# Audio tower on one core: the routing mask turned by VectorE instead of TensorE, two output pairs moved, masked experts ahead of pair additions

## The chip, the cores and the metric

The kernel runs on one core of a Trainium2 chip. The metric is the time of one execution in microseconds (us), as the device counts it; of several runs the median is given. The five engines of the core are called by the names of the profile: PE is TensorE (matrix products), PEld its loading of weights, DVE is VectorE, ACT is ScalarE, POOL is GpSimd, and SP is SyncE, which here only issues DMAs.

## What is computed

There are 16 sequences (`B`) of 374 tokens with 256 channels; a 375th row of each, the readout, is used as a second input of the first projection. For every sequence:

```python
h = gelu(x_other @ W[:256] + x_readout @ W[256:] + b)          # tok
xn = layernorm(h)                                             # attention by cosine
h = h + softmax(cosine(xn, xn)) @ xn + xn
x2 = layernorm(h)                                             # routed attention
logits = normed(x2) @ normed(sim_matrix) - sigmoid(gates)     # 8 experts
mask = logits > 0, or the two largest where none is
q = sum over experts e of mask[e] * (x2 @ q_proj[e])          # k and v alike
attn = softmax(causal(q @ k.T / sqrt(128))) @ v
h = h + sum over e of mask[e] * route_w[e] * (attn @ o_proj[e])
```

The numbers are float32. The kernel makes its products from float16 halves, three products (high x high, high x low, low x high) for each.

## The kernel before

The 374 tokens of a sequence stand as 3 tiles (`NT`) of 128 partitions, the 256 channels as 2 blocks (`NC`), and there are 8 experts (`E`). All data stays on chip; the 16 sequences go through a pipeline of stages. The order on each engine is written out by hand, and engines wait for each other on semaphores. A first part takes all sequences through the tok projection. Then `pipeline` calls `step(i, g1, f, m, n)`: in one step sequence `g1` = i+1 has its first norm, `f` = i its cosine attention, second norm and routing, `m` = i-1 its q, k and v, and `n` = i-2 its causal attention and output. The steps for f = 3 to 14 are a hardware loop, the others are written out, so that 14 steps have both an `f` and an `n`; 13 of these also have a `g1`.

What matters here, in the order of a step's second half:

- **Units.** `unit(m, which, e)` on PE is the product of expert `e` for q, k or v: six matmuls of 374 columns. A step has 24, `M(0)` to `M(23)`; 16 to 23 are those of v. The unit reads `xm[:, e]`, the tokens multiplied by the expert's mask, which `mask_tokens(f, e)` writes on DVE (L1274) for the next step once the v unit of the same expert is done. In a step of both kinds, experts 0 to 4 are masked in its end and 5 to 7 in the next one's beginning.
- **Pairs.** `pair(n, p)`, p from 0 to 11, is the output product of two experts for one tile of 128 tokens: three matmuls of 512 columns into one of two banks in turn. ACT multiplies its second half by the routing weight (`scale_pairs`, L908), after which DVE adds the first half to `h` (`add_pair`, L1180). `pair(n, p)` waits on PE until the addition of pair p-2 is done (`s_pair_added`). The twelve pairs stand between units, one at a time.
- **Route.** `logits(f)` gives the logits, `route(f)` on DVE makes the mask in 16 small instructions. It writes it as float16 into `mask16`, 8 columns in each of 3 blocks of 128 (L1261).
- **Mask around.** PE turns the mask by three transposes (`turn_mask`, L1756) between unit 15 and pair 4, ACT copies the result to `maskT` (`turned_mask`, L844), SP stores it to DRAM with one DMA (L428), waits for it, and loads it back to all 128 partitions with two DMAs (L433, experts 0 to 3 and 4 to 7) into `mask_all`, which `mask_tokens` reads.
- **POOL's work beside this.** `route_weights` (L640 to L649) needs DVE's `weight_max` and `weight_sum`; then `add_tile(n, 0)` (L663, L670, L677), then `low_1(g1)` (L624, the low half of the normed tokens, 768 elements), then `add_tile(n, 1)` and `add_tile(n, 2)`. `low_1` comes after ACT's `high(0, g1)` (L787), which in turn waits for DVE's `norm_apply_tile(0, g1, 2)` (L1159). In ACT's queue `high(0, g1)` stands ahead of the scaling of pair 7.

DVE's order in the end of a step is: additions of pairs 0 and 1, `route(f)`, pairs 2 and 3, `weight_max`, low half of k, pair 4, `weight_sum`, first norm tile of `g1`, pair 5, the other two norm tiles, pairs 6 and 7, then pair 8, masked expert 0, pair 9, expert 1, pair 10, expert 2, pair 11, experts 3 and 4.

## Time and profile before

| | |
|---|---|
| median of 3 runs | 711.19 us (710.89 to 711.81) |
| profiled execution | 711.77 us, its span of instructions 710.1 us |
| PE busy | 705.5 us, 99% of the span |
| DVE busy | 579.8 us, 82% |
| ACT busy | 378.9 us, 53% |
| POOL busy | 400.5 us, 56% |
| granted TensorE clock | 1.000 of full speed |
| a step of the loop | 40.50 us |

The span is the time from the first to the last instruction. Busy shares tell only how full an engine is; what sets the time is the chain of work in which each piece waits for the one before. Times in the rows are microseconds from the start of the span. All loop steps have the same times within it, so that the rows are taken from one of them, the step that has its unit 15 at 283.68 us.

### The profile page before, as it was taken

To read this page: it belongs to the slowest core of one execution; us is meant where nothing else is said; L and a number is where in the kernel's file an instruction comes from. 1 tells how busy PE (TensorE), PEld (TensorE's weight loads), DVE (VectorE), ACT (ScalarE), POOL (GpSimd) and SP (SyncE) were. 2 spreads that over 40 slices of the span, in tenths; PEclk is the share of its full clock that TensorE was granted. 3 is DMA by queue.
4 is the path that set the end of the run, shared out by engine and by line. 5 is a ranking of instruction groups with operands and counts; after the bars stand their busy time and mean duration, and the time that the engine had idled before them with its cause. 6 is when DMAs were issued, how large, how long until landed. Compare 5 with 4: busy or idle time off the path is not lost.

```text
span 710.1 us, 18197 instructions
## 1 busy us (share of the span) xinstructions
PE 705.5 (99%) x5440; PEld 473.1 (67%) x5440; DVE 579.8 (82%) x1455; ACT 378.9 (53%) x808; POOL 400.5 (56%) x655
## 2 busy tenths in 40 slices
PE   9999999999999999999999999999999999999998
PEld 8888666675757666575756666575766657575655
DVE  5788798888879888887979888887988888886736
ACT  4977373554646364563646355464646456364443
POOL 7652325756465566746566575746566674653434
PEclk9999999999999999999999999999999999999999
DMA  9581220202020120202020020202011020201111
GB/s 246 150 188 46 74 45 8 72 3 63 14 63 14 13 65 0 71 7 63 14 55 22 9 68 0 70 8 63 14 23 55 0 71 7 63 17 46 22 68 37
DMA packets 33558, 34.35 MB, mean 48 GB/s; under 512 B 7304, under 2 KB 29304, under 8 KB 33400
## 3 DMA queue, kind: packets, MB, share of 16 engines
q1 hardware_dynamic: 33136, 33.65, 18.4%
q8 instruction: 16, 0.26, 0.2%
q10 hardware_dynamic: 392, 0.32, 0.1%
q14 instruction: 14, 0.11, 0.1%
HBM read 27.70 MB, written 6.26 MB: 48 GB/s over the span
## 4 chain that ended last, share of the span: by engine, by line
PE 98%; issue 1%; POOL 0%; POOLq 0%; DVE 0%; ACT 0%; DVEq 0%
PE bank L1671 76%; PE bank L1734 7%; PE bank L1588 5%; PE bank L1645 3%; PE bank L1577 2%; PE bank L1805 2%; PE bank L1720 1%; PE bank L1783 1%; PE bank L1593 1%; PE bank L1612 1%; PE bank L1756 0%; PE bank L1745 0%; PE bank L1748 0%; POOL region_c L670 0%; POOL region_c L663 0%
## 5 line engine op out<-in xcount | busy, mean ns | idle before, releaser
L1671 PE MATMUL bank<-xm,w_qkv 128*128 128x374 f16 x2304 | 415.7, 322 | 0.0
L1671 PEld LDWEIGHTS bank<-xm,w_qkv 128*128 128x128 f16 x2304 | 220.8, 98 | 139.2
L908 ACT ACTIVATE region_c<-bank,out_w 128x256 f32<-128x256 f32 x180 | 84.8, 471 | 163.2 <-PE bank L1671 162.2
L1274 DVE TENSOR_TENSOR xm<-xT,mask_all 128x1496 f16<-128x1496 f16 x128 | 151.9, 1209 | 0.0
L1671 PE MATMUL bank<-w_o,aoT 128*128 128x512 f16 x540 | 143.3, 379 | 0.0
L1180 DVE SCALAR_TENSOR_TENSOR h<-bank,out_w,h 128x256 f32 (+1 forms) x180 | 86.5, 481 | 48.8 <-ACT region_c L908 43.9
L663 POOL TENSOR_TENSOR region_c<-region_c 128x512 f32<-128x512 f32 x46 | 77.1, 1675 | 27.8 <-ACT region_c L908 22.8
L692 POOL TENSOR_TENSOR exp_hl<-exp,exp_hl 128x128 f16<-128x128 f32 (+2 forms) x48 | 41.9, 875 | 83.7 <-ACT exp_hl L864 83.2
L1671 PEld LDWEIGHTS bank<-w_o,aoT 128*128 128x128 f16 x540 | 50.4, 98 | 39.5
L1159 DVE TENSOR_SCALAR region_b<-h,moments,small 128x256 f32 (+1 forms) x96 | 48.8, 553 | 6.1 <-POOL small L577 6.1
L670 POOL TENSOR_TENSOR region_c<-region_c 128x256 f32<-128x256 f32 x46 | 46.9, 1019 | 8.1 <-POOL region_c L663 7.9
L1734 PE MATMUL bank<-xhl,exp_hl 128*128 128x257 f16 (+1 forms) x432 | 50.3, 272 | 0.0
L1734 PEld LDWEIGHTS bank<-xhl,exp_hl 128*128 128x128 f16 x432 | 41.6, 97 | 7.3
L677 POOL TENSOR_TENSOR h<-region_c,h 128x256 f32 (+1 forms) x45 | 37.3, 829 | 15.2 <-POOL region_c L670 10.9
L787 ACT ACTIVATE xhl<-region_b 128x768 f16<-128x768 f32 x32 | 27.0, 844 | 33.2 <-DVE region_b L1159 33.2
L817 ACT ACTIVATE region_a<-region_a,log_p,small 128x374 f32<-128x374 f32 (+2 forms) x48 | 28.2, 587 | 26.4 <-DVE region_a L1285 26.4
L573 POOL TENSOR_SCALAR small<-moments 128x3 f32<-128x3 f32 x32 | 14.4, 449 | 49.4 <-DVE moments L1151 49.4
L1671 PE MATMUL bank<-xT 128*128 128x374 f16 (+2 forms) x288 | 37.8, 268 | 0.0
L1588 PE MATMUL bank<-w_tok,xinT 128*128 128x256 f16 x288 | 37.6, 273 | 0.0
L892 ACT ACTIVATE pT<-bank 128x768 f16<-128x768 f16 x16 | 13.0, 811 | 46.0 <-PE bank L1805 46.0
L1142 DVE BATCH_NORM_STATS2 stats<-h 128x6 f32 (+1 forms) x96 | 35.7, 413 | 0.0
L587 POOL TENSOR_TENSOR small<-small,m_half 128x3 f32<-128x3 f32 x32 | 28.3, 884 | 8.1 <-POOL small L583 8.1
(200 smaller groups left out, 1067.6 us busy)
## 6 DMA issues: line engine op xcount, KB each, us to landing
mask_all<-d_mask SPq DMA_DIRECT2D x32, 384.0 KB, 3.9
h<-in_x_dram SPq DMA_DIRECT2D x16, 256.0 KB, 5.0
out_dram<-h SPq DMA_DIRECT2D x31, 128.0 KB
rnorm_row<-d_rnorm SPq DMA_DIRECT2D x16, 192.0 KB, 4.1
h<-in_x_dram SPq DMA_DIRECT2D x15, 112.0 KB, 5.4
out_dram<-h SPq DMA_DIRECT2D x15, 112.0 KB
xm<-in_L_ffn_q_proj_dram SPq DMA_DIRECT2D x2, 512.0 KB, 7.5
region_c<-in_L_ffn_k_proj_dram SPq DMA_DIRECT2D x2, 512.0 KB, 6.4
```

The lines of the kernel that those rows point to most:

```text
L663: g.tensor_tensor(prod_sum[:, 0:2, :], prod[:, buf, 0:2, :], prod[:, buf, 2:4, :], ALU.add).then_inc(s_tile_summed, 1)
L670: g.tensor_tensor(prod_sum[:, 2, :], prod_sum[:, 0, :], prod_sum[:, 1, :], ALU.add).then_inc(s_tile_summed, 1)
L677: g.tensor_tensor(h[:, n, t, :], prod_sum[:, 2, :], h[:, n, t, :], ALU.add).then_inc(s_tile_ready, 1)
L692: done = g.tensor_tensor(exp2_hl[:, 1, sl], exp2[:, sl], exp2_hl[:, 0, sl], ALU.subtract)
L908: a.activation(prod[:, prod_buf(n, t), q, :], pair_bank(n, p)[:, C:2 * C], ACT.Copy, scale=weights_out(n)[:, t, 2 * q + 1:2 * q + 2]).then ...
L1142: v.bn_stats(stats[n][:, t, :], h[:, b, t, :]).then_inc((s_stats1, s_stats2)[n], 1)
L1159: v.tensor_scalar(xs[n][:, t, :], h[:, b, t, :], moments[n][:, t, 0:1], small[n][:, 4, t:t + 1], ALU.subtract, ALU.mult).then_inc((s_xs1, ...
L1180: v.scalar_tensor_tensor(h[:, n, t, :], pair_bank(n, p)[:, 0:C], weights_out(n)[:, t, e0:e0 + 1], h[:, n, t, :], ALU.mult, ALU.add).then_i ...
L1274: v.tensor_tensor(xm[:, e, :, 0:T], xT[1][:, :, :, 0:T].rearrange("p a c t -> p (a c) t"), mask_all[:, e, 0:T].unsqueeze(1).broadcast_to([ ...
L1588: t_.matmul(projected(t), xinT[:, b % 2, xp, c, t * P:(t + 1) * P], w_tok[:, wp, c, :], start=(c == 0 and xp == 0 and wp == 0), stop=False ...
L1671: last = t_.matmul(dst, left[lp], right[rp], start=(starts and k == 0), stop=(stops and k == 2), skip_group_check=True)
L1734: last = t_.matmul(banks[t][:, 0:n], exp1_hl[:, ep, j, t * P:(t + 1) * P], xhl[0][:, xp, j, 0:n], start=(j == 0 and k == 0), stop=(j == NT ...
```

## The change

- PE no longer turns the mask, and ACT no longer copies it. `mask16` becomes a block of 128 x 32 with the 24 values (expert, tile) of a token side by side, and DVE turns it in one instruction (`turn_mask`, a transposition of blocks of 32 x 32) into `mask_turned`, after the addition of pair 2. In it the tokens of 32 partitions stand in 24 rows of a 32-partition block.
- SP stores this with four DMAs of 24 rows with 32 values each, instead of one with 8 rows of 384 values, and then loads as before, from the same layout.
- On PE, pair 4 comes after unit 16 instead of after unit 15. Each pair after it comes a unit later too, except pair 11, which stays after unit 22 and so directly follows pair 10.
- On DVE each of the masked experts 0 to 3 comes ahead of the addition of pair 8 to 11 instead of behind it.
- The zeros for PE's first matmuls, which were in `mask16`, are now in `mask_all`.

```diff
+    SQ = 32
-        mask16 = sb("mask16", [P, NT, P], F16)
-        maskT = sb("maskT", [E, TP], F16)
+        mask16 = sb("mask16", [P, SQ], F16)
+        mask_turned = sb("mask_turned", [P, SQ], F16)
...
             def mask_around(f):
                 sp.wait_ge(s_mask_row, f + 1).then_inc(s_sp_passed, 1)
-                sp.dma_start(d_mask[f, :].rearrange("(e t) -> e t", e=E), maskT[:, :]).then_inc(s_mask_stored, 16)
-                sp.wait_ge(s_mask_stored, 16 * (f + 1)).then_inc(s_sp_passed, 1)
+                rows = d_mask[f, :].rearrange("(r b j) -> b r j", r=SQ, j=SQ)
+                for q in range(P // SQ):
+                    sp.dma_start(rows[q][0:NT * E, :], mask_turned[q * SQ:q * SQ + NT * E, :]).then_inc(s_mask_stored, 16)
+                sp.wait_ge(s_mask_stored, 16 * (P // SQ) * (f + 1)).then_inc(s_sp_passed, 1)
...
-            def turned_mask(f):
-                act.wait_ge(s_mask_turned, f + 1)
-                if later(f):
-                    act.wait_ge(s_mask_stored, 16 * f)
-                a.activation(maskT[:, :], as16(turn[1] if later(f) else turn[0], TP)[0:E, :], ACT.Copy).then_inc(s_mask_row, 1)
...
+            def turn_mask(b):
+
+                dve.wait_ge(s_mask_ready, 2 * b + 1)
+                if later(b):
+                    dve.wait_ge(s_mask_stored, 16 * (P // SQ) * b)
+                v.transpose(mask_turned[:, :], mask16[:, :]).then_inc(s_mask_row, 1)
...
                     for e in range(E - 3):
+                        mask_tokens(f, e)
                         pairs(8 + e, min(9 + e, PAIRS))
-                        mask_tokens(f, e)
...
-            def turn_mask(f):
-                pe.wait_ge(s_mask_ready, 2 * (f + 1))
-                pe.wait_ge(s_T2_lo, f + 1)
-                for t in range(NT):
-                    last = t_.transpose(as16(turn[1] if later(f) else turn[0], TP)[:, t * P:(t + 1) * P], mask16[:, t, :], ident16[:, :])
-                last.then_inc(s_mask_turned, 1)
...
-                    M(15)
-                    turn_mask(f)
+                    M(15, 16)
                     pair(n, 4)
-                    for k in range(7):
-                        M(16 + k)
+                    for k in range(6):
+                        M(17 + k)
                         pair(n, 5 + k)
+                    pair(n, PAIRS - 1)
```

PE in the loop from unit 15 on, before. The units read `xm,w_qkv` (bank1 is k, bank5 is v), the pairs `w_o,aoT`:

```order
L1671 MATMUL bank1<-xm,w_qkv 128x374 x6
L1756 MATMUL bank7<-ident16,mask16 128x128 [waits T2_lo,mask_ready]
L1756 MATMUL bank7<-ident16,mask16 128x128 x2
L1835 REGISTER_ALU
L1671 MATMUL bank2<-w_o,aoT 128x512 [waits pair_added]
L1671 MATMUL bank2<-w_o,aoT 128x512 x2
L1671 MATMUL bank5<-xm,w_qkv 128x374 [waits v_lo]
```

The same place now:

```order
L1674 MATMUL bank1<-xm,w_qkv 128x374 x6
L1674 MATMUL bank5<-xm,w_qkv 128x374 [waits v_lo]
L1674 MATMUL bank5<-xm,w_qkv 128x374 x5
L1831 REGISTER_ALU
L1674 MATMUL bank2<-w_o,aoT 128x512 [waits pair_added]
L1674 MATMUL bank2<-w_o,aoT 128x512 x2
```

The three transposes are gone, and the first v unit (bank5) stands ahead of pair 4.

PE at the end of the same loop step now, from unit 22 to the turning of the next first norm:

```order
L1674 MATMUL bank5<-xm,w_qkv 128x374 x6
L1831 REGISTER_ALU
L1674 MATMUL bank2<-w_o,aoT 128x512 [waits pair_added]
L1674 MATMUL bank2<-w_o,aoT 128x512 x2
L1831 REGISTER_ALU
L1674 MATMUL bank3<-w_o,aoT 128x512 [waits pair_added]
L1674 MATMUL bank3<-w_o,aoT 128x512 x2
L1655 REGISTER_ALU
L1649 MATMUL bank6<-ident16,xhl1 128x128 [waits logits_out,hi1]
```

Pair 10 (bank2) and pair 11 (bank3) are neighbours; before, unit 22 was between them.

DVE in the loop from the addition of pair 7, before; the additions write `h`, the masked experts `xm`:

```order
L1180 SCALAR_TENSOR_TENSOR h<-bank,out_w,h 128x256 [waits pair_added,pair_scaled]
L1177 REGISTER_ALU
L1180 ISA [waits pair_scaled]
L1180 SCALAR_TENSOR_TENSOR h<-bank,out_w,h 128x256
L1273 ISA [waits T2_lo,T2_hi,mask_loaded0]
L1274 TENSOR_TENSOR xm<-xT,mask_all 128x4x374 [waits v_done]
```

and now:

```order
L1174 SCALAR_TENSOR_TENSOR h<-bank,out_w,h 128x256 [waits pair_added,pair_scaled]
L1273 ISA [waits T2_lo,T2_hi,mask_loaded0]
L1274 TENSOR_TENSOR xm<-xT,mask_all 128x4x374 [waits v_done]
L1171 REGISTER_ALU
L1174 ISA [waits pair_scaled]
L1174 SCALAR_TENSOR_TENSOR h<-bank,out_w,h 128x256
```

The wait for the loaded mask and the first masked expert moved ahead of the addition of pair 8.

## Rows read from the trace of the kernel before

**Rows 1.** The page: busy time of each engine.

```profile
PE 705.5 (99%) x5440; PEld 473.1 (67%) x5440; DVE 579.8 (82%) x1455; ACT 378.9 (53%) x808; POOL 400.5 (56%) x655
```

**Rows 2.** One loop step: its us, busy PE, PEld, DVE, ACT, POOL, PEclk.

```profile
283.68:324.18 40.50, 40.50 (x308) 26.32 (x307) 34.49 (x88) 21.23 (x46) 24.71 (x39) 1.00 0.13 34
```

**Rows 3.** Timeline of PE: start us, us, engine, line, operation.

```profile
283.68 1.11 PE L1671 MATMUL bank<-xm,w_qkv 128*128 128x374 f16 x6
284.63 0.33 PE L1756 MATMUL bank<-ident,mask 128*128 128x128 f16 x3
284.79 0.81 PE L1671 MATMUL bank<-w_o,aoT 128*128 128x512 f16 x3
...
286.39 0.81 PE L1671 MATMUL bank<-w_o,aoT 128*128 128x512 f16 x3
...
295.98 0.81 PE L1671 MATMUL bank<-w_o,aoT 128*128 128x512 f16 x3
```

**Rows 4.** Timeline of DVE in that step: pair additions, norm tiles, masked experts.

```profile
284.21 1.07 DVE L1180 SCALAR_TENSOR_TENSOR h<-bank,out_w,h 128x256 f32 x2
...
286.41 0.49 DVE L1180 SCALAR_TENSOR_TENSOR h<-bank,out_w,h 128x256 f32 x1
...
287.75 0.48 DVE L1180 SCALAR_TENSOR_TENSOR h<-bank,out_w,h 128x256 f32 x1
288.15 1.80 DVE L1159 TENSOR_SCALAR region_b<-h,moments,small 128x256 f32 x2
...
291.22 0.48 DVE L1180 SCALAR_TENSOR_TENSOR h<-bank,out_w,h 128x256 f32 x1 [0.88 <-ACT region_c L908]
...
293.13 1.02 DVE L1274 TENSOR_TENSOR xm<-xT,mask_all 128x1496 f16<-128x1496 f16 x1
...
294.54 1.53 DVE L1274 TENSOR_TENSOR xm<-xT,mask_all 128x1496 f16<-128x1496 f16 x1
296.00 0.47 DVE L1180 SCALAR_TENSOR_TENSOR h<-bank,out_w,h 128x256 f32 x1
```

**Rows 5.** Timeline of ACT in that step.

```profile
285.07 0.48 ACT L844 ACTIVATE maskT<-bank 8x384 f16<-8x384 f16 x1 [0.72 <-PE bank L1756]
...
289.98 0.84 ACT L787 ACTIVATE xhl<-region_b 128x768 f16<-128x768 f32 x1 [0.67 <-DVE region_b L1159]
290.73 0.46 ACT L908 ACTIVATE region_c<-bank,out_w 128x256 f32<-128x256 f32 x1
```

**Rows 6.** Timeline of POOL in that step.

```profile
287.37 0.31 POOL L647 TENSOR_TENSOR lg<-lg,row 128x24 f32<-128x24 f32 x1 [1.21 <-DVE row L1345]
...
288.53 1.27 POOL L663 TENSOR_TENSOR region_c<-region_c 128x512 f32<-128x512 f32 x1 [0.34 <-POOL route_w L649]
...
291.06 0.73 POOL L677 TENSOR_TENSOR h<-region_c,h 128x256 f32 x1 [0.36 <-ACT xhl L787]
291.75 1.61 POOL L624 TENSOR_TENSOR xhl<-region_b,xhl 128x768 f16<-128x768 f32 x1
293.31 1.97 POOL L663 TENSOR_TENSOR region_c<-region_c 128x512 f32<-128x512 f32 x1
```

**Rows 7.** Timeline of DVE, early in the program.

```profile
54.35 0.55 DVE L1080 SCALAR_TENSOR_TENSOR xinT<-bank,xinT 128x384 f16<-128x384 f32 x1
```

**Rows 8.** Timeline of PE at the same place.

```profile
55.04 0.92 PE L1577 MATMUL bank<-ident,h 128*128 128x128 f32 x6
```

**Rows 9.** Timeline of SP in that step: the mask's store and its two loads.

```profile
285.79 0.30 SPq L428 DMA_DIRECT2D d_mask<-maskT  x1
287.54 0.90 SPq L433 DMA_DIRECT2D mask_all<-d_mask  x2
```

**Rows 10.** SP's waits, two steps: line, source, total us, times, longest.

```profile
SPq L420 <- DMA d_rnorm<-small: 3.9, 2, 2.2
...
SPq L429 <- DMA d_mask<-maskT: 2.5, 2, 1.3
```

**Rows 11.** DMA issues from 287.00 to 287.90: KB, us to landing.

```profile
mask_all<-d_mask SPq DMA_DIRECT2D x1, 384.0 KB, 3.7
```

More of the change, by code:

```diff
@@ L101, in audio_tower_kernel @@
         row3 = sb("row3", [P, 6, NT])
-        mask16 = sb("mask16", [P, NT, P], F16)
-        maskT = sb("maskT", [E, TP], F16)
+        mask16 = sb("mask16", [P, SQ], F16)
+        mask_turned = sb("mask_turned", [P, SQ], F16)
         mask_all = sb("mask_all", [P, E, TP], F16)
+        zeros16 = mask_all[:, 0, 0:P]
         route_w = sb("route_w", [P, B, NT, E])
@@ L160, in audio_tower_kernel @@
         d_route = nc.dram_tensor("d_route", [(NT - 1) * E * P], F32, kind="Internal").ap()
-        d_mask = nc.dram_tensor("d_mask", [B, E * TP], F16, kind="Internal").ap()
+        d_mask = nc.dram_tensor("d_mask", [B, SQ * P], F16, kind="Internal").ap()
         bank = [ctx.enter_context(nc.psum_tensor(f"bank{i}", [P, 512], F32)) for i in range(8)]
@@ L259, in audio_tower_kernel @@
         s_route_exp = sem("route_exp")
-        s_mask_turned = sem("mask_turned")
         s_mask_row = sem("mask_row")
@@ L751, in _ @@
             act.wait_ge(s_pad_zeroed, 1)
-            a.activation(unused[:, :], mask16[:, 0, 0:1], ACT.Gelu)
+            a.activation(unused[:, :], zeros16[:, 0:1], ACT.Gelu)
             def split_in(b):
@@ L920, in step @@
                     head_high(qT, qkv_bank[0], s_q_done, m + 1, s_q_hi, [], qkv_out)
-                    turned_mask(f)
                     route_exp(f)
@@ L961, in step @@
                     scale_pairs(0, 4)
-                    turned_mask(f)
                     head_high(kT, qkv_bank[1], s_k_done, m + 1, s_k_hi, [(s_scores_done, NT * m)], qkv_out)
@@ L1040, in _ @@
             exp_cosines(1, (2,))
-            turned_mask(0)
             route_exp(0)
@@ L1054, in _ @@
             v = nc.vector
-            v.memset(mask16[:, 0, :], 0.0).then_inc(s_pad_zeroed, 1)
+            v.memset(zeros16, 0.0).then_inc(s_pad_zeroed, 1)
             v.memset(h[96:P, 0:1, NT - 1, :], 0.0).then_inc(s_zeroed, 1)
@@ L1064, in _ @@
             v.memset(read_hl[:, :], 0.0).then_inc(s_zeroed, 1)
-            v.memset(mask16[:, 1:NT, :], 0.0)
+            v.memset(mask16[:, :], 0.0)
             def token_weights_low():
@@ L1258, in route @@
                                              ALU.is_lt, ALU.mult))
-                if later(b):
-                    dve.wait_ge(s_mask_turned, b)
-                v.tensor_tensor(mask16[:, :, 0:E], lg[:, 0, :, :], M, ALU.add).then_inc(s_mask_ready, 1)
+                v.tensor_tensor(mask16[:, 0:NT * E].rearrange("p (e t) -> p t e", t=NT), lg[:, 0, :, :], M,
+                                ALU.add).then_inc(s_mask_ready, 1)
                 v.tensor_tensor(lg[:, 8, :, :], lg[:, 0, :, :], M, ALU.add).then_inc(s_mask_ready, 1)
                 assert at[0] == RP
+            def turn_mask(b):
[3 more added lines that the diff above has]
+                v.transpose(mask_turned[:, :], mask16[:, :]).then_inc(s_mask_row, 1)
             def mask_tokens(b, e):
@@ L1396, in step @@
                     route(f)
+                    turn_mask(f)
                     weights_low(2 * NC)
@@ L1437, in step @@
                     route(f)
-                    pairs(2, 4)
+                    pairs(2, 3)
+                    turn_mask(f)
+                    pairs(3, 4)
                     weight_max(f)
@@ L1543, in _ @@
             route(0)
+            turn_mask(0)
             weights_low(2)
@@ L1611, in _ @@
             for k in range(WARM):
-                t_.matmul(bank[6][:, 0:P], mask16[:, 0, :], mask16[:, 0, :], start=True, stop=True)
+                t_.matmul(bank[6][:, 0:P], zeros16, zeros16, start=True, stop=True)
             pe.wait_ge(s_consts, 1)
@@ L1620, in _ @@
             for k in range(FILL):
-                t_.matmul(bank[6][:, 0:P], mask16[:, 0, :], mask16[:, 0, :], start=True, stop=True)
+                t_.matmul(bank[6][:, 0:P], zeros16, zeros16, start=True, stop=True)
             pe.wait_ge(s_tok_read, 16)
@@ L1653, in turn_first_high @@
                     pe.wait_ge(s_logits_out, b)
-                    pe.wait_ge(s_mask_row, b)
                 turn_rows(0, b, 0, turn[0], s_turned1_hi)
@@ L1929, in step @@
                     pair(n, 3)
-                    M(15)
-                    turn_mask(f)
+                    M(15, 16)
                     pair(n, 4)
-                    for k in range(7):
-                        M(16 + k)
+                    for k in range(6):
+                        M(17 + k)
                         pair(n, 5 + k)
+                    pair(n, PAIRS - 1)
                     if g1 is not None:
@@ L1946, in step @@
                 pe.wait_ge(s_logits_out, B)
-                pe.wait_ge(s_mask_row, B)
                 turn_v(n)
@@ L2023, in _ @@
             turn_in(13)
-            turn_mask(0)
             dots(1, 2)
@@ L2035, in _ @@
             pe.wait_ge(s_hi2, 2)
-            pe.wait_ge(s_mask_row, 1)
             turn_rows(1, 1, 0, turn[0], s_turned2_hi)
```

## The prediction

> **What bounds the kernel now.** I read the page first. PE is busy for 705.5 us of a span of 710.1 us [rows 1]; DVE, the next, has 82%. Busy PE in the page can hide waits, because the ends of matmuls are modelled, so I went on to the view by stages and the timeline. A loop step takes 40.50 us, in which PE is busy for 40.50 us at the full granted clock of 1.00 [rows 2]. In the timeline the starts say the same: the six matmuls of 374 columns of a unit take 0.95 us from the unit's start to what follows, wherever it stands (283.68 to 284.63), and a unit and a pair take 1.60 us together (284.79 to 286.39, and seven times that to the last pair at 295.98) [rows 3]. So PE waits for nothing in the loop. Two things follow. PE work that goes away is gained in full as long as nobody else is late, and any wait of PE that is new is lost in full.
>
> **The work taken off PE.** The three transposes stand from 284.63 to 284.79, 0.16 us [rows 3]. There are 16 such groups, one for each sequence: 16 x 0.16 = 2.56 us. I take this as it stands also for the two groups ahead of the loop, which are 0.3 us of it together. ACT loses a copy, which nobody gains by, since ACT is busy for 21.23 of 40.50 us [rows 2].
>
> **DVE's transposition.** The trace shows no such operation on DVE. The nearest rows are the small operations of 24 numbers, as POOL's L647 of 0.31 us in [rows 6]; two additions of pairs 2 and 3 with nothing between take 1.07 us together, 0.10 more than twice 0.48 [rows 4], so that up to 0.1 us of it lies in a gap and the rest delays the addition of pair 3. Even at the 0.5 us of a whole addition of 256 numbers this hits nobody: pair 3 would be added by 285.8, and pair 5, the one that waits for it on PE, now starts at 287.2. Below nothing it can't be. I take 0.2 us, because 32 numbers are nearest to the small operations. It ends at 284.21 + 0.40 + 0.2 = 284.8, where 0.40 is the distance from an addition to the next independent instruction (287.75 to 288.15) [rows 4].
>
> **The new place of the pairs.** With unit 16 in front, pair 4 starts at 284.63 + 0.95 = 285.58, and pair p at 1.60 us for each later one: pair 5 at 287.18, pair 7 at 290.37, pair 8 at 291.97, pair 9 at 293.57, pair 10 at 295.17. Pair 11 follows after 0.65 us (1.60 less 0.95) at 295.81. For pair 4 this is right: the addition of pair 2 begins at 284.21 and ends about 284.7, and left where it was, pair 4 would come at 284.63 and wait. Pairs 4 to 10 are 0.79 us later than before, and with them ACT and DVE; pair 11 is 0.17 us earlier. What decides is the last: pair 11 needs the addition of pair 9, which began on PE only 2.24 us before, where it had 3.2 us. From a pair's start on PE to the start of its addition on DVE, with ACT's scaling between, are 1.36 us (286.39 to 287.75) [rows 3, 4], to its end 1.84. PE starts 0.14 us after the end of a DVE instruction that it waited for (54.90 to 55.04) [rows 7, 8]. That makes 1.98 of 2.24 us: 0.26 us to spare, if DVE is free.
>
> **Is DVE free?** Here the exchange of masked experts and additions counts. I follow the chain through the step.
>
> The additions of pairs 4 and 5 start at 286.94 and 288.54. POOL's L647 starts 0.96 us after the first (286.41 to 287.37), L663 1.16 us later [rows 4, 6], so it wants to start at 289.06. The two norm tiles on DVE start 0.40 after pair 5's addition, at 288.94. Before, L663 came 0.38 us after the first tile had started and the second tile was held up: the pair of tiles took 1.80 us and ended at 289.95, 0.15 us after L663 (289.80) [rows 4, 6]. So these instructions of DVE and POOL's additions run one at a time. Now L663 comes 0.12 us after the first tile, waits for it till about 289.2, and ends at 290.48; the second tile ends at 290.63.
>
> POOL: L677 ends 1.99 us after L663 (289.80 to 291.79), and L624 would start 0.04 before that end [rows 6]: 292.47 and 292.43.
>
> ACT: L787 starts 0.03 us after the second tile, at 290.66, the scaling of pair 7 comes 0.75 us later (289.98 to 290.73), and DVE's addition 0.49 us after that (291.22) [rows 4, 5]: 291.90. The first masked expert is then ready to start at 292.30. It finds POOL in L677 till 292.47.
>
> A masked expert that is held up ends 0.79 us after POOL's instruction: that of 294.54 ended at 296.07, L663 at 295.28. POOL, held up by DVE, gets going about 0.14 us before DVE's end: L663 ended at 295.28, its own time of 1.27 after 294.01, and the masked expert ended at 294.15 [rows 4, 6]. So masked expert 0, which has waited longer than L624, ends at 292.47 + 0.79 = 293.26. L624 then runs its 1.61 us from 293.12 to 294.73. The addition of pair 8 does not mind that: the pair additions take 0.47 to 0.49 us whatever POOL runs [rows 4]. Masked expert 1 wants to start near 293.8, waits for L624 and ends at 294.73 + 0.79 = 295.52. The addition of pair 9, now behind it, starts 0.07 us before that end (296.00 against 296.07) [rows 4] and ends at 295.92. PE starts pair 11 at 295.92 + 0.14 = 296.06 instead of 295.81: a wait of 0.25 us.
>
> This holds in the steps that have a next first norm (L624 comes from it), 13 of them: 13 x 0.25 = 3.3 us. In the last step with a route there is none. **The sum** is 711.19 - 2.56 + 3.3 = 711.9 us. I make it against the median; the profiled execution was 711.77 us with a span of 710.1, 1.7 us around it that the change leaves alone. An error of 0.1 us in the chain is 1.3 us in the time, which makes this case 710.4 to 713.8.
>
> **The mask's way over DRAM.** Masked expert 0 can start at 292.30 only if the load has landed. Before, the first store came 0.24 us after ACT's copy had ended (285.55 to 285.79) [rows 5, 9]; now it comes at 284.8 + 0.24 = 285.05. Issues of one kind are 0.5 us apart (two loads of about 0.35 took 0.90) [rows 9], so the fourth store is issued at 286.55. From a store's issue to the load's is 1.75 us (285.79 to 287.54), and the load lands 3.7 us later [rows 9, 11]: 292.0, 0.4 us before L624. The bound above is the store of the norms, 128 short rows: SP waits for it 2.2 us at the longest, for the mask's 1.3 us [rows 10]. The new stores have 24 rows of 64 bytes each, before 8 of 768. At 0.9 us more the load lands at 292.9, too late. Four small stores at once are nearer to the mask's store in rows than to that of the norms, so I take 292.0 to 292.2.
>
> The Trainium skill says in "DMA: Bandwidth & Descriptors", under Specifications, that a transfer below 512 bytes makes the DMA engine read, modify and write. That speaks against this change; by it the four stores would be slower than the row, and the case would be the second rival below. No row of before shows a store of the mask in 64-byte pieces.
>
> **First rival, PE waits for nothing.** If the masked experts 0 and 1 don't meet L624 between them, say since it keeps out of DVE's way, each takes the 0.9 to 1.0 us of an undisturbed one, the addition of pair 9 ends at 293.57 + 1.84 = 295.41, and pair 11 starts on time. Then the whole 2.56 us are gained: 708.6 us. For it: the chain has a dozen steps, and 0.26 us in it are enough. Against it: the two norm tiles and the masked expert of 294.54 were held up by POOL in just this way [rows 4], in every step of the loop.
>
> **Second rival, the load comes too late, slower.** If masked expert 0 is not ready when POOL comes to L624 at 292.43, L624 takes its turn first, till 294.04. Masked expert 0 ends at 294.83, and the addition of pair 8, which now stands behind it, at 295.23; pair 10 starts at 295.37 instead of 295.17, 0.20 late. POOL's L663 goes ahead of masked expert 1 (294.69 to 295.96), which ends at 296.75; the addition of pair 9 ends at 297.15, and pair 11 starts at 297.29 instead of 296.01, 1.28 late. Together 1.48 us in each of 13 steps, 19.2 us: 711.19 - 2.56 + 19.2 = 727.8 us. The point from which it decides is a landing about 0.4 us later than I have it. For it: the 64-byte rows and four issues where one was. Against it: the transposition and PE's and ACT's copy that no longer stand ahead give 0.7 us back.
>
> That the change does not do what it says, that is that PE's 0.16 us don't come free, has nothing for it in a PE that is full, and gets no share of its own.
>
> **How the numbers follow.** The forecast's case, 711.9 us, has 0.55; the first rival, 708.6, has 0.25; the second, 727.8, has 0.20. The range leaves out the second rival and nothing else: 708.3 to 714.5. A measurement of this kernel can tell 0.2%, 1.4 us, from no change: faster is below 709.8, slower above 712.6. Of the likeliest case 0.36 lies between, 0.17 above and 0.02 below. Of the first rival 0.23 is faster and 0.02 within. That makes 0.25 faster, 0.38 the same, 0.37 slower.
>
> **What the profile after would show.** Right: a loop step of 40.50 - 0.16 + 0.25 = 40.6 us; a gap on PE only ahead of the last pair, with DVE's addition as its releaser; the first masked expert of a step ending ahead of L624 and the second held up by it; unit 15 and unit 16 next to each other without a gap. First rival: a step of 40.34 us and no gap. Second: a step near 41.8 us, and L624 ahead of the first masked expert. The prediction is wrong if PE waits at another place, say at pair 4 or at the first units of the next step, if the order of DVE and POOL at 292.4 is another, or if PE does not give 0.16 us for each mask.

## The result: slower by 1.1%, outside the range

| | before | after |
|---|---|---|
| median of 5 runs | 711.81 us (710.89 to 712.2) | 719.94 us (718.95 to 719.99) |
| ratio | | 1.0112, 95% interval 1.01 to 1.0124 |
| profiled execution, span | 711.77, 710.1 us | 719.03, 717.3 us |
| forecast | | 711.9 us, 708.3 to 714.5 |

The change costs 8.1 us between the medians and 7.2 us between the two spans. The page of after, against [rows 1]:

```profile
PE 705.8 (98%) x5392; PEld 468.9 (65%) x5392; DVE 587.6 (82%) x1471; ACT 374.4 (52%) x792; POOL 400.6 (56%) x655
```

48 matmuls are gone, and busy PE still shows 0.3 us more. As in before, that number hides waits. Two neighbouring loop steps by stages, columns as in [rows 2]:

```profile
286.86:327.40 40.54, 40.50 (x305) 26.09 (x303) 34.32 (x89) 20.96 (x45) 24.95 (x39) 1.00 0.14 34
327.40:369.16 41.76, 40.66 (x305) 26.00 (x303) 35.82 (x89) 20.96 (x45) 24.04 (x39) 1.00 0.13 33
```

In before one step of the loop was as long as the next. Now there are two kinds, of 40.54 and of 41.76 us, at the same granted clock and with the same number of instructions. The forecast named 40.6 us for its own case and "near 41.8" for the second rival: both came true, in one execution. PE's waits by source (us in total, times, longest) point to one place:

```profile
PEld bank L1674 <- DVE h L1174: 15.4, 20, 1.6
```

L1174 is the addition of a pair. The waits of PEld overlap matmuls that still run, so I take PE's own gaps from the starts of matmuls, less the time of their columns. Below, T is the start of DVE's transposition in a step: 286.73 in the first of these two, 327.26 in the second.

**A short step.** PE from pair 9, DVE and POOL:

```profile
295.68 0.81 PE L1674 MATMUL bank<-w_o,aoT 128*128 128x512 f16 x3
296.32 1.11 PE L1674 MATMUL bank<-xm,w_qkv 128*128 128x374 f16 x6
297.27 1.67 PE L1674 MATMUL bank<-w_o,aoT 128*128 128x512 f16 x6
298.78 0.39 PE L1649 MATMUL bank<-ident,xhl 128*128 128x128 f16 x4
...
294.04 0.48 DVE L1174 SCALAR_TENSOR_TENSOR h<-bank,out_w,h 128x256 f32 x1 [0.88 <-ACT region_c L905]
294.44 0.97 DVE L1274 TENSOR_TENSOR xm<-xT,mask_all 128x1496 f16<-128x1496 f16 x1
295.63 0.48 DVE L1174 SCALAR_TENSOR_TENSOR h<-bank,out_w,h 128x256 f32 x1 [0.22 <-ACT region_c L905]
296.03 1.64 DVE L1274 TENSOR_TENSOR xm<-xT,mask_all 128x1496 f16<-128x1496 f16 x1
297.59 0.47 DVE L1174 SCALAR_TENSOR_TENSOR h<-bank,out_w,h 128x256 f32 x1
...
293.88 0.73 POOL L680 TENSOR_TENSOR h<-region_c,h 128x256 f32 x1 [0.36 <-ACT xhl L790]
294.57 2.31 POOL L627 TENSOR_TENSOR xhl<-region_b,xhl 128x768 f16<-128x768 f32 x1
```

Pairs 10 and 11 stand from 297.27 to 298.78, 1.51 us, where two pairs of 0.65 take 1.30: the gap ahead of pair 11 is 0.21. Masked expert 0 starts at 294.44, ahead of POOL's L627 (L624 in before). L627 is held up by it and takes 2.31 us instead of 1.61; masked expert 1 is held up by L627 and takes 1.64; the addition behind it ends at 298.06, and pair 11 follows.

**A long step**, the same three engines:

```profile
336.22 0.81 PE L1674 MATMUL bank<-w_o,aoT 128*128 128x512 f16 x3
336.87 1.11 PE L1674 MATMUL bank<-xm,w_qkv 128*128 128x374 f16 x6
337.96 0.82 PE L1674 MATMUL bank<-w_o,aoT 128*128 128x512 f16 x3
339.89 0.82 PE L1674 MATMUL bank<-w_o,aoT 128*128 128x512 f16 x3 [1.10 <-DVE h L1174]
...
334.58 0.48 DVE L1174 SCALAR_TENSOR_TENSOR h<-bank,out_w,h 128x256 f32 x1 [0.88 <-ACT region_c L905]
335.35 2.16 DVE L1274 TENSOR_TENSOR xm<-xT,mask_all 128x1496 f16<-128x1496 f16 x1 [0.28 <-DMA mask_all<-d_mask]
337.43 0.47 DVE L1174 SCALAR_TENSOR_TENSOR h<-bank,out_w,h 128x256 f32 x1
337.83 1.60 DVE L1274 TENSOR_TENSOR xm<-xT,mask_all 128x1496 f16<-128x1496 f16 x1
339.36 0.47 DVE L1174 SCALAR_TENSOR_TENSOR h<-bank,out_w,h 128x256 f32 x1
...
334.43 0.72 POOL L680 TENSOR_TENSOR h<-region_c,h 128x256 f32 x1 [0.36 <-ACT xhl L790]
335.11 1.61 POOL L627 TENSOR_TENSOR xhl<-region_b,xhl 128x768 f16<-128x768 f32 x1
336.68 1.97 POOL L666 TENSOR_TENSOR region_c<-region_c 128x512 f32<-128x512 f32 x1
```

Masked expert 0 now waits for the DMA that brings the mask, and POOL's L627 starts first, undisturbed (1.61). The masked expert takes 2.16 us, pair 10 starts 0.15 late (336.22 + 1.59 would be 337.81), and pair 11, 0.65 after pair 10 without a wait, comes 1.27 late.

**Which step is which kind.** By the trace the first of the two loads has landed 7.34 to 7.64 us after T in the 7 short steps and 7.74 to 7.97 in the 5 long ones of the loop. L627 comes at 7.83 to 7.86 in either; a masked expert starts about 0.1 us behind its wait. The two kinds don't overlap. The first step with both parts, ahead of the loop (T = 122.37), has the long order too, but not for the mask's sake. Its mask landed 7.01 us after T, and DVE came to the masked expert only at 7.70, when POOL had begun at 7.57:

```profile
130.07 2.27 DVE L1274 TENSOR_TENSOR xm<-xT,mask_all 128x1496 f16<-128x1496 f16 x1
...
129.94 1.61 POOL L627 TENSOR_TENSOR xhl<-region_b,xhl 128x768 f16<-128x768 f32 x1
```

Pair 11 waits 1.06 us there. Seven gaps of 0.20, five of 1.42 and this one of 1.06 make 1.4 + 7.1 + 1.1 = 9.6 us. Less the 2.56 us of the transposes, and with 0.2 us of gaps in the program's first part, this is 7.2 us, what the spans differ by. Runs of after lie at 718.95 to 719.03 and at 719.94 to 719.99; one long step in place of a short one is 1.2 us, which fits the distance of 0.96 roughly, but only one of these runs has a trace.

SP in the two steps, the short one first:

```profile
285.93 0.37 SPq L424 DMA_DIRECT2D rnorm_row<-d_rnorm  x1
287.17 1.82 SPq L431 DMA_DIRECT2D d_mask<-mask_turned  x4
290.52 0.95 SPq L436 DMA_DIRECT2D mask_all<-d_mask  x2
...
327.04 0.37 SPq L424 DMA_DIRECT2D rnorm_row<-d_rnorm  x1
327.71 1.82 SPq L431 DMA_DIRECT2D d_mask<-mask_turned  x4
331.49 0.95 SPq L436 DMA_DIRECT2D mask_all<-d_mask  x2
```

The stores start 0.44 us after T in both, as forecast (284.61 to 285.05). The loads are issued 3.79 and 4.23 us after T; over all steps it is 3.69 to 4.36, where the forecast has 3.69 for every step (288.30). L424 is the load of the norms' row, 192 KB, on the same queue just ahead of the stores. It lands 2.73 to 3.37 us after T, and in the loop steps the loads of the mask are issued 0.96 to 1.01 us behind that landing. In before the same thing varied too; the loads in two other loop steps:

```profile
247.42 0.90 SPq L433 DMA_DIRECT2D mask_all<-d_mask  x2
...
328.13 0.90 SPq L433 DMA_DIRECT2D mask_all<-d_mask  x2
```

Counted from PE's transposes (244.13, 284.63 and 325.13) these and [rows 9] are 3.29, 2.91 and 3.00 us. Over all loop steps of before it is 2.92 to 3.45, and in eleven of the twelve the loads go out 0.13 to 0.19 us behind the landing of the norms' row; in the twelfth, where that row was issued late (0.45 us behind the transposes), they go out 0.10 ahead of it. The forecast took its row from one step, and the section on the profile before said that all loop steps have the same times. That holds for the four engines that compute, not for DMAs.

### The profile page after: what moved, and what is told of

Its sections match the earlier page's. It is cut to its first block, busy times and chain, and to the rows that moved or that the text cites. A ratio compares the mean times of both kernels' runs of the same rounds, so it can differ in the third digit from the quotient of the medians.

```text
span 717.3 us, 18200 instructions
## 1 busy us (share of the span) xinstructions
PE 705.8 (98%) x5392; PEld 468.9 (65%) x5392; DVE 587.6 (82%) x1471; ACT 374.4 (52%) x792; POOL 400.6 (56%) x655
## 4 chain that ended last, share of the span: by engine, by line
PE 94%; DVE 2%; issue 2%; ACT 1%; POOL 1%; POOLq 0%; DVEq 0%; ACTq 0%
PE bank L1674 74%; PE bank L1737 7%; PE bank L1592 4%; PE bank L1649 3%; PE bank L1801 1%; PE bank L1581 1%; PE bank L1723 1%; PE bank L1779 1%; PE bank L1616 1%; PE bank L1597 1%; DVE h L1174 1%; ACT region_c L905 1%; DVE xm L1274 0%; PE bank L1751 0%; PE bank L1748 0%
## 5 line engine op out<-in xcount | busy, mean ns | idle before, releaser
L1274 DVE TENSOR_TENSOR xm<-xT,mask_all 128x1496 f16<-128x1496 f16 x128 | 158.8, 1255 | 1.0 <-DMA mask_all<-d_mask 0.8
L1174 DVE SCALAR_TENSOR_TENSOR h<-bank,out_w,h 128x256 f32 (+1 forms) x180 | 86.2, 479 | 45.5 <-ACT region_c L905 44.0
L695 POOL TENSOR_TENSOR exp_hl<-exp,exp_hl 128x128 f16<-128x128 f32 (+2 forms) x48 | 38.9, 811 | 74.1 <-ACT exp_hl L861 74.0
L627 POOL TENSOR_TENSOR xhl<-region_b,xhl 128x768 f16<-128x768 f32 x16 | 31.0, 1940 | 4.5 <-ACT xhl L790 4.5
```

What stands on the lines that cost most here:

```text
L695: done = g.tensor_tensor(exp2_hl[:, 1, sl], exp2[:, sl], exp2_hl[:, 0, sl], ALU.subtract)
L1174: v.scalar_tensor_tensor(h[:, n, t, :], pair_bank(n, p)[:, 0:C], weights_out(n)[:, t, e0:e0 + 1], h[:, n, t, :], ALU.mult, ALU.add).then_i ...
L1274: v.tensor_tensor(xm[:, e, :, 0:T], xT[1][:, :, :, 0:T].rearrange("p a c t -> p (a c) t"), mask_all[:, e, 0:T].unsqueeze(1).broadcast_to([ ...
```

## The experiments

All have the median of their batch's runs of before beside them: 711.51, 711.6, 711.52 and 711.58 us for the four batches.

### Which part of the change costs: e4, e5, e1

**e4** turns the mask on DVE and leaves the pairs and the masked experts in the order of before.

```diff
-                    M(15, 16)
+                    M(15)
                     pair(n, 4)
-                    for k in range(6):
-                        M(17 + k)
+                    for k in range(7):
+                        M(16 + k)
                         pair(n, 5 + k)
-                    pair(n, PAIRS - 1)
...
-                        mask_tokens(f, e)
                         pairs(8 + e, min(9 + e, PAIRS))
+                        mask_tokens(f, e)
```

> Only the turning of the mask is changed: on DVE instead of PE and ACT, with four stores. The pairs stand on PE as in the kernel before (pair 4 behind unit 15, unit 22 between pairs 10 and 11), and DVE's order of additions and masked experts is that of before. Theory: the only wait is that of pair 4 for the addition of pair 2, which ends 0.06 us after pair 4 could start, 0.2 us with the distance from DVE to PE, in 14 steps: 711.8 - 2.56 + 0.2 + 2.8 = 712.2 us. Rival (the four stores themselves cost the time, by coming late for the masked experts wherever the pairs stand): gaps at pairs 9 to 11 too, 716 us or more.

Measured: 710.87 us, ratio 0.9991 (0.9981 to 1.0001). PE's waits for additions:

```profile
PEld bank L1674 <- DVE h L1174: 4.7, 15, 0.3
```

Pair 4 waits 0.13 us in each loop step, as it comes 0.16 earlier and the addition of pair 2 hasn't ended; nothing else waits. 711.5 - 2.56 + 12 x 0.13 + 0.2 is 710.7. That is below the expected 712.2: PE starts 0.06 us after the end of the addition, not 0.14, and the steps outside the loop have no such wait. So PE does give back 0.16 us for each mask, and none of the 8 us of loss comes from DVE's turning or from the four small stores by themselves.

**e5** is the kernel before with only the masked experts ahead of the additions:

```diff
                     for e in range(E - 3):
+                        mask_tokens(f, e)
                         pairs(8 + e, min(9 + e, PAIRS))
-                        mask_tokens(f, e)
```

> The kernel before with one part of the change alone: masked experts 0 to 3 ahead of the additions of pairs 8 to 11 on DVE; the mask is turned by PE and the pairs stand as before. Theory: the load lands 0.5 us ahead of L624, masked expert 0 goes first, and the addition of pair 9 ends near 10.6 us after the transposes, while pair 11 can start at 11.35 at the soonest: no wait on PE, 711.5 us, no change within 0.1%. Rival (the exchange costs time by itself, wherever the pairs stand): 0.2 us or more in each of 13 steps, 714 us or more.

Measured: 712.01 us (711.34 to 712.93), ratio 1.0005 (0.9996 to 1.0015): no change that can be told from none, as expected. Its trace is not quite free of cost, though. In eleven of the loop steps PE has no gap; in the one in which the mask lands at 7.16 us after the transposes, with L624 at 7.12, POOL goes first and pairs 10 and 11 wait 0.23 and 0.31 us. The first step with both parts loses 0.28, with its mask in time. The exchange thus brings the race in by itself; with the pairs in their old places losing it costs 0.5 us instead of 1.4.

**e1** is after with that exchange undone, so that the pairs stand late and the additions first.

```diff
-                        mask_tokens(f, e)
                         pairs(8 + e, min(9 + e, PAIRS))
+                        mask_tokens(f, e)
```

> The changed kernel with one part undone: on DVE the additions of pairs 8 to 11 stand ahead of masked experts 0 to 3 again. Theory (masked experts 0 and 1 stand ahead of the additions of pairs 8 and 9 and are held up by POOL's L624): the addition of pair 9 then waits for masked expert 0 alone, is done about 10.8 us after the step's transposition, and pair 11, due at 11.2, finds it done. No gap on PE in the loop, a step of 40.34 us, about 709.4 us in all (711.8 less 2.56, and 0.2 us that the changed kernel shows more in its first part). Rival (pair 11 is simply too close behind pair 9, whatever DVE does first): the gaps ahead of pair 11 stay, 717 us or more.

Measured: 720.97 us, ratio 1.0131 (1.0115 to 1.0148), a miss of 11.6 us. The gaps of pair 11 are gone but for 0.37 us in the first step, as expected. In their place two others stand in every loop step (waits, then PEld in one step):

```profile
PEld bank L1723 <- DVE exp_hl L1295: 11.4, 15, 0.9
...
PEld bank L1674 <- DVE region_a L1285: 4.8, 14, 0.4
```

```profile
305.45 0.32 PEld L1674 LDWEIGHTS bank<-xT 128*128 128x128 f16 x6 [0.37 <-DVE region_a L1285]
...
308.83 0.23 PEld L1723 LDWEIGHTS bank<-ident,exp_hl 128*128 128x128 f16 x4 [0.88 <-DVE exp_hl L1295]
```

PE loses 0.13 to 0.16 us ahead of the cosines' third product and 0.67 to 0.69 ahead of the turning of the exponentials. The additions end on time, the masked experts behind them don't, and DVE carries its backlog into the next step. Once the pairs stand 0.8 us later either order costs PE something: 0.8 us a step in this one, 0.2 in that of the change as long as the mask is in time. The exchange is thus the cheaper order.

### What makes a step long: e2, e3

Both move only DVE's turning: e2 directly behind the route, ahead of pair 2's addition, e3 behind the addition of pair 3.

```diff
                     route(f)
+                    turn_mask(f)
                     pairs(2, 3)
-                    turn_mask(f)
```

> The changed kernel with the transposition on DVE ahead of the addition of pair 2 instead of behind it, so that the mask sets out about 0.4 us earlier. Theory (a step is of the long kind when the mask's load lands after POOL has come to L624, of the short kind when before; landings were 7.35 to 7.97 us after the transposition, L624 comes at 7.84): all 13 steps are of the short kind with 0.2 us of wait, 711.8 - 2.56 + 0.2 + 13 x 0.2 = 712.0 us. Rival (the two kinds come from something that builds up over the steps, such as the store of the previous output): both kinds remain, 717 to 720 us.

Measured: 714.13 us, ratio 1.0037 (1.0024 to 1.005), with the profiled execution at 717.38. Three loop steps in it are long, not none: their masks landed 8.02 to 8.16 us after their T, L627 came at 8.10, and the nine short ones landed by 7.95.

```diff
                     pairs(2, 3)
-                    turn_mask(f)
...
+                    turn_mask(f)
```

> The changed kernel with the transposition behind the addition of pair 3, about 0.6 us later. Theory (race between the mask's load and L624): all 13 steps are of the long kind, 1.42 us each (1.06 in the first), 711.8 - 2.56 + 0.2 + 12 x 1.42 + 1.06 = 727.5 us. Rival (the two kinds come from something else than the load's time): 718 to 720 us as before.

Measured: 720.65 us, ratio 1.0124 (1.0097 to 1.0151); six loop steps are long, not twelve. Landings of 6.93 to 7.13 us after T are in the short ones, 7.17 to 7.40 in the long ones, L627 at 7.25 to 7.28.

Both runs miss in their number and confirm the race: in both a step is long when the mask lands later than about 0.1 us ahead of L627. (Both also have the first step's 1.06 us with the mask in time.) The misses have one cause. In e3 the norms' row has landed by 2.46 us after T in all loop steps but one, and in these the loads are issued at a fixed 3.46 to 3.48. In e2 it lands at 2.93 to 3.41, and the loads go out 0.98 to 1.0 later, at 3.92 to 4.40. A turning that is 0.26 earlier thus buys much less than 0.26, and one that is later loses less than expected, as its stores stood behind the row for less time.

### The queue of the norms' row and the four stores: e9, e7

**e9** has SP issue the load of the norms' row behind the loads of the mask.

```diff
-                    norms_in(g)
...
                     mask_around(f)
...
+                if g is not None:
+                    norms_in(g)
```

> The changed kernel with SP's load of the norms' row (192 KB to all partitions) behind the mask's stores and loads instead of ahead of them. Theory B (the mask's stores land about 1.0 us after that load): without it ahead, the mask's load is issued at a fixed 3.46 us after the transposition (1.5 us after the fourth store), as in e3_turn_late, lands at 7.2 to 7.4, ahead of L624 at 7.84, and all 13 steps are of the short kind: 712.0 us. Theory A (the four issues and the short rows alone): no difference, both kinds remain, 717 to 720 us.

Measured: 712.79 us, ratio 1.0015 (1.0005 to 1.0025). All twelve loop steps are short, with gaps of 0.19 to 0.22 us. SP in a step with T = 285.62:

```profile
286.06 1.79 SPq L431 DMA_DIRECT2D d_mask<-mask_turned  x4
289.05 0.94 SPq L436 DMA_DIRECT2D mask_all<-d_mask  x2
290.37 0.33 SPq L424 DMA_DIRECT2D rnorm_row<-d_rnorm  x1
```

From the first store to the loads are 2.99 us, where after had 3.35 and 3.78 in the two steps above, and the loads are issued 3.42 to 3.44 us after T in every loop step. The spread is gone with the norms' row. The first step keeps its 1.06 us.

**e7** keeps the norms' row ahead and stores the mask with one DMA, the 8 unused rows of each block with it:

```diff
-                for q in range(P // SQ):
-                    sp.dma_start(rows[q][0:NT * E, :], mask_turned[q * SQ:q * SQ + NT * E, :]).then_inc(s_mask_stored, 16)
-                sp.wait_ge(s_mask_stored, 16 * (P // SQ) * (f + 1)).then_inc(s_sp_passed, 1)
+                sp.dma_start(rows, mask_turned[:, :]).then_inc(s_mask_stored, 16)
+                sp.wait_ge(s_mask_stored, 16 * (f + 1)).then_inc(s_sp_passed, 1)
```

> The changed kernel with one store of the whole turned mask (128 rows of 32 values) instead of four of 24 rows. Theory A (the store is late because the fourth issue is 1.5 us behind the first): it lands about 1.5 us earlier, all 13 steps are of the short kind, 712 us. Theory B (the store lands about 1.0 us after the load of the norms' row that SP issued before it on the same queue, at 2.7 to 3.2 us after the transposition, whatever its own issue time): both kinds of step remain, 716 to 720 us.

Measured: 712.78 us, ratio 1.0015 (1.0005 to 1.0024), again all twelve short.

```profile
284.70 0.37 SPq L424 DMA_DIRECT2D rnorm_row<-d_rnorm  x1
286.09 0.61 SPq L429 DMA_DIRECT2D d_mask<-mask_turned  x1
288.89 0.90 SPq L434 DMA_DIRECT2D mask_all<-d_mask  x2
```

The loads go out 2.79 to 3.45 us after T, 0.33 to 0.39 behind the landing of the norms' row (2.42 to 3.11), in one loop step 0.13 behind it. The loads behind four stores come 0.6 us later relative to the row. So both count, the queue and the number of issues, and either one taken away is enough. The loss against before falls from 8.1 us to 1.2 (711.6 - 2.56 + 12 x 0.2 + 1.06 + 0.2 is 712.7).

The Trainium skill says in "DMA: Bandwidth & Descriptors", under Queues, rings and completion order, that a DMA's increment of its semaphore lands only after every earlier write of the same DMA engine, across its queues. The runs agree in most steps: the mask's loads, which wait for the stores, go out 0.96 to 1.01 us behind the landing of the norms' row with four stores and 0.13 to 0.39 with one (e7). It is no order between whole DMAs, though: in one loop step of before the loads went out 0.10 us ahead of that landing. Why four stores take 0.6 more than one is not told by it, and stays open.

### Who has to go first: e8, e12

In both, POOL makes the low half of the next sequence's tokens in the loop for 32 of 256 channels only; the rest of that half is left out.

```diff
-                g.tensor_tensor(xhl[0][:, 1, :, 0:C], xs[0][:, :, :], xhl[0][:, 0, :, 0:C],
+                wide = 32 if not isinstance(b, int) else C
+                g.tensor_tensor(xhl[0][:, 1, :, 0:wide], xs[0][:, :, 0:wide], xhl[0][:, 0, :, 0:wide],
```

> The changed kernel, in which POOL's L624 of the loop's steps takes 32 of the 256 channels of each tile instead of all (7 of 8 parts of the first norm's low half are left out, stale numbers stand in their place). It then takes 0.4 us instead of 1.6. Theory (the long kind of step is L624 going ahead of masked expert 0, with its full length): POOL's next addition L666 takes L624's place between masked experts 0 and 1, so the short kind keeps its 0.2 us, but a mask that lands late costs no more than 0.4 us. No gap above 0.4 us in the 12 steps of the loop, 712 to 713.5 us. Rival (a late mask by itself makes DVE late, POOL has nothing to do with it): gaps of 1.27 us in about half of the steps, 717 us or more.

e8 gave 712.6 us, ratio 1.0018 (1.0008 to 1.0027), with no gap over 0.26 us in the loop. By itself this proves little: in its profiled execution no mask of the loop was late (7.08 to 7.70 us after T, POOL's low half at 7.84 to 7.87). So **e12** adds e3's late turning, which had made six steps long.

> The kernel e3_turn_late (transposition behind the addition of pair 3; its mask landed after or within 0.1 us of L624 in every loop step, 6 of 12 of them long) with L624 of the loop's steps cut to 32 of 256 channels, as in e8_short_L624 (7 of 8 parts of the first norm's low half are left out). In e8_short_L624 all masks of the profiled execution landed in time, so that it did not show what a late one costs. Theory (a late mask is dear because POOL takes 1.6 us of L624 first): a mask up to 0.3 us later than L624 now waits only 0.4 us for it, the addition of pair 9 then comes as in a short step, and the long kind becomes rare: gaps of 0.2 to 0.4 us, 712 to 715 us. Rival (lateness of the load alone makes the long step): as e3_turn_late, about 720 us.

(Of e3's masks not all were that late: in three loop steps they landed 0.28 to 0.32 us ahead of L627.)

Measured: 712.9 us, ratio 1.002 (1.001 to 1.003), where e3 had 720.65. Four masks landed at 7.21 to 7.44 us after T, with POOL's L628 at 7.25; one of these steps (T = 286.02), DVE and POOL:

```profile
293.36 1.09 DVE L1275 TENSOR_TENSOR xm<-xT,mask_all 128x1496 f16<-128x1496 f16 x1
...
293.28 0.36 POOL L628 TENSOR_TENSOR xhl<-region_b,xhl 128x96 f16<-128x96 f32 x1
```

POOL goes first here too, but holds up the masked expert for only a tenth of a us, and pair 11 waits 0.18. In the four steps with a late mask it waits 0.17 to 0.27, as much as in the others. A late mask costs 1.4 us only with a long POOL instruction to let in. That part of the second rival is shown.

### A version that beats both: e6, e10, e11

**e6** gives pair 11 its distance back: PE does it behind the turning of the next first norm, ahead of unit 23, and ACT's scaling follows the same order.

```diff
-                    pair(n, PAIRS - 1)
...
+                    pair(n, PAIRS - 1)
                     M(23)
...
-                    scale_pairs(7, PAIRS)
+                    scale_pairs(7, PAIRS - 1)
...
+                    scale_pairs(PAIRS - 1, PAIRS)
```

> The changed kernel with pair 11 on PE behind the turning of the next first norm (12 transposes, 0.66 us) instead of directly behind pair 10; ACT copies the turned rows ahead of scaling pair 11. Theory: in a step of the short kind pair 9's addition is done 0.4 us before pair 11 comes, no wait; in one of the long kind pair 10 waits 0.15 us and pair 11 0.7. With 6 long steps of 13 about 714 us. Rival (after e1_adds_first, in which pair 11 did not wait but the next step did: DVE is the bound of a step whose pairs are 0.8 us late, and any time saved here comes back at the beginning of the next step): gaps ahead of the third product of the cosines or the turning of its exponentials, 717 us or more.

Measured: 710.66 us (709.61 to 711.76), ratio 0.9987 (0.9978 to 0.9997), better than the expected 714. Its profiled execution had no gap in the loop, a step of 40.33 us and 0.39 us in the first step; but its masks had all landed in time there (7.0 to 7.6 us after T). What a late mask costs in this order is not shown; the 2 us between its fastest and its slowest run may be one or two of them, but no trace shows it.

**e10** is e6 with e9's order and e7's store, so that the mask is in time always.

> The changed kernel with three edits together: pair 11 behind the turning of the next first norm (as in e6_pair11_apart), the norms' row loaded behind the mask (as in e9_norms_behind), one store for the mask (as in e7_one_store). Theory: no gap in the loop in any execution, a step of 40.33 us, at most 0.4 us in the first step: 711.6 - 2.56 + 0.2 + 0.4 = 709.6 us, and less spread between runs than the 709.6 to 711.8 us of e6_pair11_apart, whose spread came from single long steps. Rival (that spread is of the chip, not of the mask's way): the same median as e6_pair11_apart, 710.7 us.

Measured: 709.58 us (708.93 to 710.4 in 8 runs), ratio 0.9973 (0.9962 to 0.9983), 2 us below before, as expected. Waits and a loop step:

```profile
PEld bank L1674 <- DVE h L1174: 1.0, 3, 0.4
```

```profile
284.50:324.83 40.33, 40.33 (x305) 26.17 (x304) 34.29 (x89) 21.05 (x46) 24.98 (x39) 1.00 0.11 34
```

This is 40.50 - 0.16 with no gap at all, what the first rival promised for the loop: 711.5 - 2.56 + 0.4 + 0.2 is 709.5.

**e11** tried e4 the other way: pair 2's addition inside the route, between two of its comparisons, and the turning directly behind it.

```diff
-                v.tensor_tensor(square[1], others, mine, ALU.is_equal)
+                between()
...
-                    route(f)
-                    pairs(2, 3)
+                    route(f, lambda: pairs(2, 3))
```

> The kernel e4_turn_only (mask turned by DVE, pairs and additions in the order of before) with the addition of pair 2 moved up into the route, behind its second comparison, and the transposition directly behind the route. Theory: pair 4's wait of 0.13 us in 12 steps goes, since pair 2 is added 1.5 us sooner than pair 4 needs it, and the route ends at most 0.4 us later, which nobody waits for: no gap in the loop, 711.6 - 2.56 + 0.2 = 709.2 us. Rival (the later mask meets L624 as in the changed kernel, or DVE is late for pairs 3 and 5): 710.5 us or more.

Measured: 711.46 us, ratio 0.9999 (0.999 to 1.0008), a miss. Pair 4's gap is gone, and one of 0.13 to 0.145 us stands ahead of the turning of the next step's exponentials:

```profile
PEld bank L1725 <- DVE exp_hl L1298: 4.4, 13, 0.4
```

It is the place where e1 lost its 0.7 us. I take it that here too DVE carries work over the boundary of two steps, since in e11 masked expert 0 takes 1.22 us, where in e4 it takes 0.94; no run tests that.

## Why the prediction failed

- **PE gives back 0.16 us for each mask:** right. e4 and e10 show it, and the step of 40.33 us.
- **DVE's transposition, 0.2 us, without harm:** right; it took 0.200 to 0.211 us:

```profile
L1263 DVE STREAM_TRANSPOSE mask_turned<-mask x16: 200/202/211, 52.0 to 656.4; 128x32 f16<-128x32 f16 x16
```

- **The forecast's case, the chain through DVE and POOL to pair 11:** right where it applied. The gap was 0.20 to 0.22 us against 0.25, in 7 of 13 steps. Counted from the transposition, pair 9's addition was forecast to end at 11.31 us and ended at 11.33. The 0.05 that are left are the step from DVE to PE: the forecast took 0.14 from a float32 transpose [rows 7, 8], and ahead of the pairs it is 0.06 (298.06 to 298.12). The sum took all 13 steps as alike, but the first, with its mask in time, loses 1.06 us and not 0.25, since POOL is at its low half 0.13 us before DVE is at masked expert 0. With the mask in time in all loop steps (e7, e9) the kernel takes 712.8 us, inside the range.
- **The second rival's mechanism and price:** right. 0.15 and 1.27 us late against 0.20 and 1.28, POOL's low half ahead of masked expert 0.
- **The mask's way over DRAM:** this is the step that failed. It put the landing at 292.0 to 292.2, 7.4 to 7.6 us after T, and POOL's low half at 7.82, from one step's 1.75 us between store and load and 3.7 us from load to landing. That is where the short steps are (7.34 to 7.64); it is no value for all, which go up to 7.97: from the last store to the loads were 1.73 to 2.39 us, from there to the landing 3.4 to 3.9. The bound of 0.9 us for the store covered this, but the forecast looked for the risk in the 64-byte rows. Those don't show, as the last section has it. What it missed is the queue, which was in its own row already: in before the 1.75 us were the shortest of the loop (1.75 to 2.28), and outside the loop, where no norms' row stands ahead, the loads follow the store by 1.35 to 1.44. Without the norms' row the loads would go out 3.43 us after T; behind it they go out 0.26 to 0.93 later, by an amount that differs from step to step.
- **The sum:** "13 x 0.25" and "1.48 us in each of 13 steps" took the two cases as one or the other for the whole program. With a landing that varies by 0.6 us from step to step against a deadline (about 7.74) 0.15 to 0.35 us behind the value taken, the mixture was the likeliest case, and the range left it out. The loads of before, 2.92 to 3.45 us after the transposes, showed that spread. By the forecast's own prices, 7 steps of 0.25 and 6 of 1.48 are 719.3 us; that this meets the 719.94 so well is part luck, as one of the six is the first step, which the mask did not make long. Of the distance, 0.6 us are before itself, 711.19 in the forecast and 711.81 beside the result. Two slips change nothing: 0.1 us in 13 steps around 711.9 is 710.6 to 713.2, not 710.4 to 713.8, and three groups of transposes stand ahead of the loop, not two; the 2.56 us count them all.
- **The rule on 512 bytes,** which the forecast had from the Trainium skill ("DMA: Bandwidth & Descriptors", Specifications): it was to speak for the second rival. The second rival came, but not by that: e7 and e9 still store rows of 64 bytes, and all their loop steps are short.

What stays open is why the norms' row lands at 2.7 us in one step and at 3.4 in another (it was issued 0.23 to 1.04 us ahead of T and took 3.43 to 4.25), and why runs of the same kernel differ in it.

## To carry over

When a change moves a small DMA forward, look at what stands ahead of it on its queue, not only at when its data is ready: it may move up to the tail of a large transfer and wait there. Where two engines race for a turn and the loser pays much more than the winner, take the arrival from all steps of the trace, not from one, and price the mixture. And two products of which the second waits until a busy engine is done with the one before need their distance kept: moving one pair behind other PE work (e6) was worth 9 us here against the change as made, and 2 us against the versions whose mask is in time (e7, e9).

## What the runs showed of the hardware

- Four small stores on SP's queue behind a load of 192 KB to 128 partitions let the DMA that waits for them go out 0.96 to 1.01 us after that load has landed; with one store of 128 rows (e7) it is 0.33 to 0.39 us, with one of 8 rows (before) 0.13 to 0.19, but for one loop step of each.
- Who starts first decides between DVE and POOL, and by the whole instruction. L627 took 1.61 us alone and 2.31 behind a masked expert; the masked expert 0.97 alone and 2.16 behind L627. The Trainium skill says in "SBUF — State Buffer", under Who interferes with whom, that a `tensor_tensor` of DVE with both inputs in SBUF contends with GpSimd's reads, and that the order of issue decides who blocks. The traces agree, and a difference of 0.1 us in arrival became 1.2 us of time.
- Rows of 64 bytes in place of 768 made no difference that could be seen to the mask's store of 6 KB. In the steps outside the loop no norms' row stands ahead; one of before, then one of after:

```profile
650.06 0.30 SPq L428 DMA_DIRECT2D d_mask<-maskT  x1
651.48 0.84 SPq L433 DMA_DIRECT2D mask_all<-d_mask  x2
...
656.68 1.54 SPq L431 DMA_DIRECT2D d_mask<-mask_turned  x4
659.31 0.84 SPq L436 DMA_DIRECT2D mask_all<-d_mask  x2
```

  From the store of 8 rows of 768 bytes to the loads are 1.42 us. The last of the four stores of 24 rows of 64 bytes was issued at 657.85, 1.46 us ahead of the loads; in e9's loop it is 1.50 to 1.52, in the two other such steps of after 1.37 and 1.86. One store of 128 rows of 64 bytes (8 KB) takes longer: 2.28 to 2.30 us in e10's loop.
- PE starts 0.06 us after the end of the pair addition that it waited for; ahead of the float32 transposes of the first part it is 0.14 to 0.15.
